# The edge stage of a four-layer convolution network: operators, normalisation and first convolution as one 5x5 convolution per image on raw input

## Chip, cores and metric

One core of one Trainium2 chip runs the kernel. The metric is the device time of one execution in microseconds. TensorE (PE) multiplies, VectorE (DVE), ScalarE (ACT) and GpSimd (POOL) work elementwise, SyncE (SP) issues most of the transfers.

## What is computed

The whole network maps x, 16 images of 32 channels of 128 x 128 float32, through four layers, each `x + layer(group_norm(x))`. The change touches the start of layer 3. There, v is the normalised x, and per image:

```
b1 = norm(sobel(v)); b2 = norm(scharr(v)); b3 = norm(laplace(v))
b4 = norm(roberts(v)); b5 = norm(prewitt(v))      # each channel by itself, reflect padding
y  = concat(b1..b5)                                # 160 channels
y  = conv3x3(y, conv1_w, conv1_b)                  # zero padding, 32 channels
y  = maxpool2(y)
...                                                # the hourglass, up to orig * y
def norm(x): return (x - mean(x)) / std(x)         # over channels, rows and columns of one image
```

## The kernel before, in words

`program` runs stages one after the other, each in a block of its own with a barrier at its end: per layer a `norm_table` (scale and shift of every channel of every image) and the layer's stages. What concerns us are the last five: `norm_table` "n2", `conv_layer` "l2" (layer 2, tensor names `l_`), `norm_table` "n3", `edges` ("l3a") and `hourglass` ("l3b"). Earlier stages give rows to compare: layer 0 (`l_mx`, `l_pv`), `state_space` (`l1m`), `tap_rows` (`l1y`), `deform` (`l1d`).

`norm_table` loads an image of 2 MB after the other (L74), takes statistics on VectorE (`bn_stats`, L87), and at the end one small matmul, a root and a store of the table (L76). GpSimd has nothing to do in it.

`edges` works through the 16 images in a hardware loop. Per image SyncE loads strips of 16 rows three times, shifted by one row each, onto 96 partitions (`xb`); ScalarE normalises them (`xn`, L1990 to L1994). TensorE makes the operator maps chunk by chunk of 4 rows: three matmuls with `w4` for four operators on 128 partitions (`p4`), three with `w5` for the fifth on 96 partitions (`p5`), L2103, 32 chunks. ScalarE and VectorE copy them to `r4` and `r5` (L2005, L2007, L2044, L2046) and VectorE takes statistics (L2047, L2049). After the last chunk comes a chain of small operations for mean and deviation; then ScalarE scales all of `r5` in place (L2018) and VectorE all of `r4` (L2079). Only then TensorE convolves: 8 steps of 12 taps, each tap four matmuls that write 32 partitions each side by side (L2118). VectorE takes the 2 x 2 maximum of each step (L2082), adds the bias (L2087), and SyncE stores the pooled rows. Every engine takes its instructions in the order in which they are written; semaphores are the only ordering between engines.

## Time and profile before

| | us |
|---|---|
| median of 3 runs | 24395.71 (24389.47 to 24419.06) |
| the profiled execution, its time | 24396.36 |
| its span, first to last instruction | 24394.8 |
| TensorE busy in the span | 19768.2 (81%) |
| VectorE busy | 15076.5 (62%) |
| ScalarE busy | 13799.3 (57%) |
| GpSimd busy | 8849.7 (36%) |

Busy shares are averages over stages that have different limits, so they have to be read stage by stage. Rows of the profile name line, engine, operation and "output <- inputs" with the tensors' names; PEld is TensorE loading weights, SPq and POOLq are queues of transfers, PEclk is the granted TensorE clock as a share of 2.4 GHz. Timeline rows begin with start and length in us. Sequences of "xN" are N instructions in a row.

### The profile page before, as it was taken

The page shows a single profiled execution, that of the slowest core. Times are in us where ns is not written, and L with a number is a line of the kernel's source. Part 1 is how long each engine was busy: PE and PEld are TensorE (multiplying, and loading weights), DVE is VectorE, ACT ScalarE, POOL GpSimd, SP SyncE. Part 2 cuts the span into 40 slices and gives each one's busy share as a digit, 9 for nine tenths or more (in the row PEclk, how much of TensorE's full clock was granted, in tenths as well). Part 3 has the DMA queues.
Part 4 walks back from the last instruction along what each step waited for, and adds up shares of the span by engine and source line. Part 5 has one row for each costly group of instructions (what it writes and reads, how often), then busy time and mean ns, then how long its engine had stood idle before and what let it go on. Part 6 is the DMA issues. An engine that isn't in the chain of part 4 may idle for free. (4 is left out here: it accounts for less than half of the span.)

```text
span 24394.8 us, 385684 instructions
## 1 busy us (share of the span) xinstructions
PE 19768.2 (81%) x135184; PEld 8014.9 (33%) x135184; DVE 15076.5 (62%) x15737; ACT 13799.3 (57%) x22826; POOL 8849.7 (36%) x5553
## 2 busy tenths in 40 slices
PE   6888888886438888888868999994468888888999
PEld 2333333332112222222215555551123333333444
DVE  8999999998138888888855666564143333333011
ACT  6889999896336666666636877783322222222111
POOL 6777778785017777777750000000000000000000
PEclk9999999998769999999988998797789999999999
DMA  1000000001950000000022111126920000111011
GB/s 65 11 12 12 11 12 12 12 11 64 158 116 18 18 18 18 18 17 18 18 69 35 34 34 37 30 38 151 198 71 23 23 23 23 29 24 30 31 43 43
DMA packets 1301498, 995.53 MB, mean 41 GB/s; under 512 B 748392, under 2 KB 1157584, under 8 KB 1265112
## 3 DMA queue, kind: packets, MB, share of 16 engines
q1 hardware_dynamic: 1199560, 849.64, 16.3%
q0 software_dynamic: 26624, 100.67, 1.5%
q10 hardware_dynamic: 74448, 33.14, 0.5%
q8 instruction: 608, 9.96, 0.2%
q14 instruction: 258, 2.11, 0.0%
HBM read 771.60 MB, written 211.63 MB: 40 GB/s over the span
## 5 line engine op out<-in xcount | busy, mean ns | idle before, releaser
L270 DVE TENSOR_TENSOR l_mx<-l_p_v,l_puN 128x2048 f32<-128x2048 f32 x2560 | 5636.5, 2282 | 151.6 <-PE l_p_s L485 138.7
L485 PE MATMUL l_p_s<-l_mx,l_w2z 128*32 128x512 f32 x32768 | 3827.9, 611 | 579.8 <-ACT l_mx L397 315.3
L290 POOL TENSOR_TENSOR l_mx<-l_pv,l_puP 128x2048 f32<-128x2048 f32 x1024 | 3715.6, 3644 | 321.8 <-PE l_p_s L485 316.0
L2103 PE MATMUL l3a_p<-l3a_xn,l3a_w 128*128 128x512 f32 (+1 forms) x6144 | 2680.9, 599 | 271.1 <-ACT l3a_xn L1994 271.1
L1157 DVE TENSOR_TENSOR_SCAN l1m_hs<-l1m_da,l1m_carry,l1m_pu 128x512 f32<-128x512 f32 x2304 | 2824.4, 1268 | 105.9 <-ACT l1m_da L1073 2.2
L2209 POOL DMA_DIRECT2D l3b_xt<-x_after x64 | 33.9, 529 | 7644.3 <-DVE l3b_most L2338 5818.0
L1206 POOL TENSOR_TENSOR l1m_hc<-l1m_hs,l1m_cs 128x1024 f32<-128x1024 f32 x1152 | 2708.7, 2351 | 9.2 <-DVE l1m_hs L1157 5.7
L1815 ACT ACTIVATE l1d_ab<-l1d_pt 128x1024 f32<-128x1024 f32 x2304 | 2299.4, 1024 | 706.9 <-PE l1d_pt L1569 693.0
L416 ACT ACTIVATE l_mx<-l_pv,l_puP 128x128 f32<-128x128 f32 x8192 | 2446.8, 393 | 0.8
L1693 DVE TENSOR_SCALAR l1d_hat<-l1d_ab 128x1024 f32<-128x1024 f32 x2304 | 1623.0, 704 | 818.9 <-ACT l1d_ab L1815 516.4
L397 ACT ACTIVATE l_mx<-l_mx 128x2048 f32<-128x2048 f32 x1024 | 1954.4, 1909 | 49.5 <-POOL l_mx L290 48.9
L485 PEld LDWEIGHTS l_p_s<-l_mx,l_w2z 128*32 128x32 f32 x32768 | 984.6, 112 | 3020.9 <-issue 1760.6
L1147 DVE TENSOR_TENSOR l1m_pu<-l1m_pu,l1m_bs 128x512 f32<-128x512 f32 x2304 | 1477.5, 687 | 749.3 <-PE l1m_pu L902 749.0
L1073 ACT ACTIVATE l1m_da<-l1m_pr,l1m_an 128x512 f32<-128x512 f32 x2304 | 1457.2, 683 | 823.4 <-PE l1m_pr L895 772.8
L902 PE MATMUL l1m_pu<-l1m_dts,l1m_sl 32*128 32x512 f32 x4608 | 1420.7, 692 | 534.8 <-ACT l1m_da L1073 525.9
L2231 PE MATMUL l3b_ps<-l3b_in,l3b_wc 128*128 (+2 forms) x3888 | 1638.2, 583 | 127.7 <-DMA l3b_in<-pooled 102.9
L2103 PEld LDWEIGHTS l3a_p<-l3a_xn,l3a_w 128*128 128x128 f32 (+1 forms) x6144 | 1094.1, 178 | 1857.9 <-issue 1857.9
L1604 PE MATMUL l1d_po<-l1d_hat,l1d_ring 128*32 128x128 f32 x36864 | 1640.6, 300 | 49.8 <-DVE l1d_hat L1693 45.8
L2118 PE MATMUL l3a_pc<-l3a_r,l3a_c 128*32 128x512 f32 x12288 | 1357.7, 605 | 270.7 <-issue 270.7
L1877 POOL TENSOR_TENSOR l1d_res<-l1d_res,l1d_xr 128x512 f32<-128x512 f32 x128 | 168.7, 1319 | 3540.6 <-ACT l1d_res L1824 3540.6
L895 PE MATMUL l1m_pr<-l1m_dts,l1m_sl 32*128 32x512 f32 x4608 | 1407.8, 689 | 2.7 <-ACT l1m_da L1073 2.7
L2005 ACT ACTIVATE l3a_r<-l3a_p 128x512 f32<-128x512 f32 x512 | 306.3, 598 | 1810.2 <-PE l3a_p L2103 1810.2
(301 smaller groups left out, 26624.6 us busy)
## 6 DMA issues: line engine op xcount, KB each, us to landing
n_xt<-x_after SPq DMA_DIRECT2D x48, 2048.0 KB
l3a_xb<-x_after SPq DMA_DIRECT2D x352, 256.0 KB, 4.1
...
l1m_sq<-seq SPq DMA_DIRECT2D x256, 144.0 KB
...
l_xs<-in_x_dram SPq DMA_DIRECT2D x128, 256.0 KB, 2.9
x_after<-l_ot SPq DMA_DIRECT2D x128, 256.0 KB, 2.4
```

The lines of the kernel that those rows point to most:

```text
L270: v.tensor_tensor(mx[:, r % QB, :, :, :], columns.unsqueeze(1).broadcast_to([P, 4, G, P]), rows.broadcast_to([P, 4, G, P]), ALU.max).then_ ...
L290: g.tensor_tensor(mx[:, r % QB, :, :, :], pv[:, u, :, :].unsqueeze(1).broadcast_to([P, 4, G, P]), rows.broadcast_to([P, 4, G, P]), ALU.add ...
L397: act.activation(tile, tile, ACT.Relu).then_inc(max_by_g, 1)
L416: ins = act.activation(mx[:, r % QB, q, t, :], pv[:, u, t, :], ACT.Relu, bias=puP[:, u, t, R * q + r:R * q + r + 1])
L485: ins = pe.matmul(p_s[R * q:R * (q + 1), 512 * u:512 * (u + 1)], w2z[:, 31 - r:63 - r], mx[:, r % QB, q, :, :].rearrange("p t v -> p (t v) ...
L1157: dve.tensor_tensor_scan(hs[:, p % 3, part, :], da[:, p % 3, part, :], pu[:, LC * bank:LC * (bank + 1)], carry[:, u, c:c + 1], ALU.mult, A ...
L1206: g.tensor_tensor(hc[:, (3 * u + p) % 6], hs[:, p % 3], cs[:, u:u + 1, :].broadcast_to([NB, 2, LC]), ALU.mult).then_inc(hc_done, 2)
L1604: ins = pe.matmul(po[C * g:C * (g + 1), 512 * (s % 2):512 * (s % 2) + P], ring[:, (8 * u + s + k) % RING, g, k, :], hat[:, m % 3, n % 2, P ...
L1693: v.tensor_scalar(hat[:, m % 3], ab[:, m % 2], 1.0, 1.0, ALU.min, ALU.subtract).then_inc(hat_done, 1)
L1815: act.activation(ab[:, m % 2].rearrange("p a n -> p (a n)"), pt[:, 1024 * (m % 2):1024 * (m % 2 + 1)], ACT.Abs).then_inc(abs_done, 1)
L2103: ins = pe.matmul(acc[0:n, 512 * (ch % 2):512 * (ch % 2 + 1)], w[:, dx, :], xn[:, k % 2, r:r + RC, dx:dx + W], start=dx == 0, stop=dx == 2)
L2231: ins = pe.matmul(bank(name, u, rows * size), wc[:, k, tap, :], src[:, at((i + u) * rows + tap // 3, rows), tap % 3:tap % 3 + size], start ...
```

## The change

Normalising the maps and convolving them is linear, and so are the operators, so all of it is one 5 x 5 convolution of the raw x per image, with taps that depend on the image through five standard deviations and the scale of x. Per image the taps are a weighted sum of five fixed tap tensors, one per operator.

- `norm_table` gets an option: GpSimd makes the fixed taps out of `conv1_w` and operator coefficients while the table is computed, three operators in "n2", two in "n3", and SyncE stores them (`folded`, 49 matrices of 32 columns per operator).
- `edges` is written anew. `xs` holds the raw image four times, shifted by 0 or 1 row and 0 or 1 column, so that a matmul over 128 partitions covers 2 x 2 taps: nine matmuls, four abreast, make a step (`pc`, 8 steps per image). Pixels of the outer rim follow other taps and are computed apart in `bb` (`border`), copied to `side` and `ends`, and put in place of the rim of each step before the maximum.
- The statistics of the five maps no longer fall out of TensorE's maps. They come from the *next* image beside the convolution of this one: its rows are loaded in strips (`xe`), 4 rows of each quarter on 128 partitions, normalised by ScalarE (`xn`), differenced by GpSimd (`tv`, `th`, `tp`, `t1`, `t2`, `te`, `tg`) and VectorE (`td`, `tf`, `t3`), made into five maps by VectorE with their sums, and squared by ScalarE with sums of the squares. Eight chunks make an image.
- After the last chunk: one small matmul, a root, and VectorE's `weights`, which forms the image's 49 matrices (`wb`, 1568 columns).

The core of the diff (loads of weights, the rim's matmuls and copies, and what is removed are left out; the removed part is `edges` as printed above):

```diff
+                g.wait_ge(f_in, 32)
+                step = 0
+                for i in range(F):
+                    for t in range(9):
+                        weight = ft[:, i, t, :].unsqueeze(1).broadcast_to([P, ROUNDS, T])
+                        coef = fc[:, i, t, :].unsqueeze(2).broadcast_to([P, ROUNDS, T])
+                        g.tensor_tensor(fv[:, i] if t == 0 else fp[:, t % 2], weight, coef, ALU.mult).then_inc(f_step, 1)
+                        step += 1
+                        if t > 0:
+                            g.wait_ge(f_step, step)
+                            g.tensor_tensor(fv[:, i], fv[:, i], fp[:, t % 2], ALU.add).then_inc(f_step, 1)
+                            step += 1
+
         @block.tensor
...
+def edges(nc, x, table, folded, taps, valid, mean_image, bias, out, B):
...
+            def strips(i, c):
+                n = i * NB + c
+                if not (isinstance(n, int) and n < 2):
+                    sp.wait_ge(xn_ready, n - 1)
...
+            def refill(i, k):
+                if not isinstance(i, int) or i > 0:
+                    sp.wait_ge(conv_done, i * NB + (min(max(k + 1, 2), NB - 1) + 1 - NB))
...
+            def once(b, u, follows, two_follow):
+                after, second = b + 1, b + 2
+                if follows:
+                    for c in range(2, 6):
+                        strips(after, c)
+                    refill(after, 0)
+                    strips(after, 6)
+                    refill(after, 1)
+                    strips(after, 7)
+                    refill(after, 2)
+                    if two_follow:
+                        strips(second, 0)
+                    refill(after, 3)
+                    if two_follow:
+                        strips(second, 1)
+                    for k in range(4, NB):
+                        refill(after, k)
...
+            def normalised(i, c, p):
+                n, u = i * NB + c, c % 2
+                if c == 0:
+                    act.wait_ge(g_ready, i + 1)
+                act.wait_ge(xe_in[u], xe_arrived(i, c))
+                if not (isinstance(n, int) and n < 2):
+                    act.wait_ge(pool_chunk, n - 1)
+                    act.wait_ge(dve_chunk, n - 1)
+                scale, shift_ = gcur[:, p, 0:1], gcur[:, p, 1:2]
+                act.activation(xn[:, u, :, 1:W + 1], xe[:, u], ACT.Identity, scale=scale, bias=shift_)
+                act.activation(xn[:, u, :, 0:1], xe[:, u, :, 1:2], ACT.Identity, scale=scale, bias=shift_)
+                act.activation(xn[:, u, :, W + 1:W + 2], xe[:, u, :, W - 2:W - 1], ACT.Identity, scale=scale, bias=shift_).then_inc(xn_ready, 1)
...
+            def squares(i, c):
+                u = c % 2
+                act.wait_ge(dve_chunk, i * NB + (c + 1))
+                for o in range(OPS):
+                    ins = act.activation(maps[:, u, o, :], maps[:, u, o, :], ACT.Square, accum_out=acc[:, OPS + o, c:c + 1])
+                ins.then_inc(sq_done, 1)
...
+            def once(b, u, follows, two_follow):
+                for k in range(5, NB):
+                    fix(b, k)
+                if follows:
+                    squares(b + 1, 0)
+                    normalised(b + 1, 2, 1 - u)
+                    squares(b + 1, 1)
+                    normalised(b + 1, 3, 1 - u)
+                border(b, u)
+                if follows:
+                    for c in range(2, 5):
+                        squares(b + 1, c)
+                        normalised(b + 1, c + 2, 1 - u)
+                    fix(b + 1, 0)
+                    squares(b + 1, 5)
+                    normalised(b + 1, 7, 1 - u)
+                    fix(b + 1, 1)
+                    squares(b + 1, 6)
+                    fix(b + 1, 2)
+                    squares(b + 1, 7)
+                    if two_follow:
+                        normalised(b + 2, 0, u)
+                        normalised(b + 2, 1, u)
+                    deviation(b + 1)
+                    fix(b + 1, 3)
+                    fix(b + 1, 4)
...
+            def chunk(i, c):
+                n, u = i * NB + c, c % 2
+                px = lambda dy, dx, rows=CR: xn[:, u, 1 + dy:1 + dy + rows, 1 + dx:1 + dx + W]
+                g.wait_ge(xn_ready, n + 1)
+                if not (isinstance(n, int) and n < 1):
+                    g.wait_ge(pool_chunk, n)
+                g.tensor_tensor(tv[:], px(1, 0), px(-1, 0), ALU.subtract)
+                g.tensor_tensor(th[:], px(0, 1), px(0, -1), ALU.subtract).then_inc(pool_first, 1)
+                if not (isinstance(n, int) and n < 2):
+                    g.wait_ge(dve_chunk, n - 1)
+                g.tensor_tensor(tp[:, u], px(-1, -1, CR + 1), px(-1, 0, CR + 1), ALU.add)
+                g.tensor_tensor(t1[:, u], px(-1, -1), px(1, 1), ALU.add)
+                g.tensor_tensor(t2[:, u], px(-1, 1), px(1, -1), ALU.add)
+                g.wait_ge(pool_first, n + 1)
+                g.tensor_tensor(te[:, u], tv[:], th[:], ALU.add)
+                g.tensor_tensor(tg[:, u], th[:], tv[:], ALU.subtract).then_inc(pool_chunk, 1)
...
+            def chunk(i, c):
+                n, u = i * NB + c, c % 2
+                px = lambda dy, dx: xn[:, u, 1 + dy:1 + dy + CR, 1 + dx:1 + dx + W]
+                to = lambda o: maps[:, u, o, :].rearrange("p (y x) -> p y x", x=W)
+                v.wait_ge(xn_ready, n + 1)
+                if not (isinstance(n, int) and n < 1):
+                    v.wait_ge(dve_chunk, n)
+                v.tensor_tensor(td[:], px(1, 1), px(-1, -1), ALU.subtract)
+                v.tensor_tensor(tf[:], px(-1, 1), px(1, -1), ALU.subtract)
+                v.wait_ge(pool_chunk, n + 1)
+                v.tensor_tensor(t3[:], t1[:, u], t2[:, u], ALU.add).then_inc(dve_first, 1)
+                if not (isinstance(n, int) and n < 2):
+                    v.wait_ge(sq_done, n - 1)
+                v.scalar_tensor_tensor(out=to(3), in0=tp[:, u, 0:CR], scalar=-1.0, in1=tp[:, u, 1:CR + 1], op0=ALU.mult, op1=ALU.add,
+                                       accum_out=acc[:, 3, c:c + 1])
+                v.wait_ge(dve_first, n + 1)
+                v.scalar_tensor_tensor(out=to(0), in0=td[:], scalar=1.0, in1=te[:, u], op0=ALU.mult, op1=ALU.add, accum_out=acc[:, 0, c:c + 1])
+                v.scalar_tensor_tensor(out=to(1), in0=td[:], scalar=0.6, in1=te[:, u], op0=ALU.mult, op1=ALU.add, accum_out=acc[:, 1, c:c + 1])
+                v.scalar_tensor_tensor(out=to(2), in0=px(0, 0), scalar=-4.0, in1=t3[:], op0=ALU.mult, op1=ALU.add, accum_out=acc[:, 2, c:c + 1])
+                v.scalar_tensor_tensor(out=to(4), in0=tf[:], scalar=2.0, in1=tg[:, u], op0=ALU.mult, op1=ALU.add,
+                                       accum_out=acc[:, 4, c:c + 1]).then_inc(dve_chunk, 1)
...
+            def weights(i, p):
+                v.wait_ge(dev_ready, i + 1)
...
+                v.tensor_scalar(wb[:, p, :], fv[:, 0, :], coef[:, 0:1], None, ALU.mult).then_inc(chain, 1)
...
+                for o in range(1, OPS):
+                    v.wait_ge(chain, i * CHAIN + (7, 8, 10, 11)[o - 1])
+                    ins = v.scalar_tensor_tensor(out=wb[:, p, :], in0=fv[:, o, :], scalar=coef[:, o:o + 1], in1=wb[:, p, :],
+                                                 op0=ALU.mult, op1=ALU.add).then_inc(w_ready if o == OPS - 1 else chain, 1)
...
+            def pool(b, k):
+                bank = pc[:, 512 * (k % 4):512 * (k % 4 + 1)]
+                v.wait_ge(conv_done, b * NB + (k + 1))
...
+                rows = bank.rearrange("p (y x) -> p y x", x=W)
+                v.tensor_copy(rows[:, :, 0:W:W - 1], side[:, k]).then_inc(replaced, 1)
...
+                v.tensor_reduce(pooled[:, k, :].rearrange("p (a w) -> p a w", w=W // 2),
+                                bank.rearrange("p (a dy x dx) -> p a x dy dx", a=CR // 2, dy=2, dx=2), AX.XY, ALU.max).then_inc(pool_done, 1)
...
+            def once(b, u, follows, two_follow):
+                if two_follow:
+                    choose(b + 2, u)
+                if follows:
+                    for c in range(4):
+                        chunk(b + 1, c)
+                for k in range(4):
+                    pool(b, k)
+                    if follows:
+                        chunk(b + 1, 4 + k)
+                pool(b, 4)
+                if follows:
+                    totals(b + 1)
+                pool(b, 5)
+                if follows:
+                    spread(b + 1)
+                    weights(b + 1, 1 - u)
+                pool(b, 6)
+                pool(b, 7)
+                v.wait_ge(pool_done, b * NB + NB + 4)
...
+            def step(b, u, k):
+                pe.wait_ge(fixed, b * NB + (k + 1))
+                pe.wait_ge(pool_done, b * NB + (k + 1))
+                rounds = rounds_of(KINDS[0])
...
+                        r, j = 16 * k + CR * g + by + 2, bx + 2
+                        ins = pe.matmul(pc[C * g:C * (g + 1), 512 * (k % 4):512 * (k % 4 + 1)], weight(u, n), xs[:, r:r + CR, j:j + W],
+                                        start=n == 0, stop=n == len(rounds) - 1, tile_position=(0, C * g))
...
+            def once(b, u, follows, two_follow):
+                pe.wait_ge(w_ready, b + 1)
+                step(b, u, 0)
+                step(b, u, 1)
+                border(b, u)
+                for k in range(2, 6):
+                    step(b, u, k)
+                if follows:
+                    total(b + 1)
+                step(b, u, 6)
+                step(b, u, 7)
```

Of GpSimd before, from the end of `deform` on, the whole list up to `hourglass`: none of it lies in the edge stage. Below, its last elementwise work, in `deform`, as the list of before has it, and then the transfers of `hourglass`:

```order
L1877 TENSOR_TENSOR l1d_res<-l1d_res,l1d_xr 128x512 x3
L1883 TENSOR_TENSOR l1d_finished<-l1d_eps 128x1
L1866 DMA x_after<-l1d_res 128x16x128
L1430 UNCONDITIONAL_BRANCH
L24 ISA x5
L2203 UNCONDITIONAL_BRANCH
L2205 UNCONDITIONAL_BRANCH
L2206 UNCONDITIONAL_BRANCH
L2206 ISA
L2209 ISA
L2209 DMA l3b_xt<-x_after 128x1024
```

Now, in the edge stage, one chunk (there are 8 per image; `l3a_xn` is the normalised strip):

```order
L2203 TENSOR_TENSOR l3a_tv<-l3a_xn 128x512
L2204 TENSOR_TENSOR l3a_th<-l3a_xn 128x512
L2207 TENSOR_TENSOR l3a_tp<-l3a_xn 128x640
L2208 TENSOR_TENSOR l3a_t<-l3a_xn 128x512
L2209 TENSOR_TENSOR l3a_t<-l3a_xn 128x512
L2211 TENSOR_TENSOR l3a_te<-l3a_tv,l3a_th 128x512
L2212 TENSOR_TENSOR l3a_tg<-l3a_th,l3a_tv 128x512
```

GpSimd received seven two-input operations per chunk, all from SBUF.

VectorE in the edge stage before, one chunk of 4 rows (32 per image; `l3a_p` is PSUM):

```order
L2044 COPY l3a_r<-l3a_p 32x4x128
L2046 COPY l3a_r<-l3a_p 32x4x128
L2047 BN_STATS l3a_parts<-l3a_p 32x6
L2048 REGISTER_ALU
L2049 BN_STATS l3a_parts<-l3a_r 128x6
```

Now VectorE in the loop over images, one pooling of this image and one chunk of the next:

```order
L2297 COPY l3a_pc<-l3a_side 128x4x2
L2304 REGISTER_ALU
L2305 TENSOR_REDUCE l3a_pooled<-l3a_pc 128x128
L2242 REGISTER_ALU
L2245 TENSOR_TENSOR l3a_td<-l3a_xn 128x512
L2246 TENSOR_TENSOR l3a_tf<-l3a_xn 128x512
L2248 TENSOR_TENSOR l3a_t<-l3a_t 128x512
L2251 SCALAR_TENSOR_TENSOR l3a_maps,l3a_acc<-l3a_tp 128x512
L2254 SCALAR_TENSOR_TENSOR l3a_maps,l3a_acc<-l3a_td,l3a_te 128x512
L2255 SCALAR_TENSOR_TENSOR l3a_maps,l3a_acc<-l3a_td,l3a_te 128x512
L2256 SCALAR_TENSOR_TENSOR l3a_maps,l3a_acc<-l3a_xn,l3a_t 128x512
L2257 SCALAR_TENSOR_TENSOR l3a_maps,l3a_acc<-l3a_tf,l3a_tg 128x512
```

The copies out of PSUM are gone; eight operations with both inputs in SBUF stand in their place, and the poolings moved in between them.

ScalarE before, two of the 32 chunks of an image, the copies of the maps out of PSUM:

```order
L2005 ACTIVATE l3a_r<-l3a_p 128x4x128
L2007 ACTIVATE l3a_r<-l3a_p 32x4x128
L2002 REGISTER_ALU
L2005 ACTIVATE l3a_r<-l3a_p 128x4x128
L2007 ACTIVATE l3a_r<-l3a_p 32x4x128
```

Now ScalarE where one image's statistics end and the next one's begin: squares of chunk 6, the columns of one refill (`xs`), squares of chunk 7, chunk 0 of the image after:

```order
L2127 ACTIVATE l3a_maps,l3a_acc<-l3a_maps 128x512 x5
L2139 ACTIVATE l3a_xs<-l3a_xs 64x16x2 x2
L2125 REGISTER_ALU
L2127 ACTIVATE l3a_maps,l3a_acc<-l3a_maps 128x512 x5
L2113 REGISTER_ALU
L2114 ISA
L2116 ISA
L2119 ACTIVATE l3a_xn<-l3a_xe,l3a_gcur 128x6x128
L2120 ACTIVATE l3a_xn<-l3a_xe,l3a_gcur 128x6
L2121 ACTIVATE l3a_xn<-l3a_xe,l3a_gcur 128x6
```

The copies are gone, and the squares of chunk 7 stand ahead of the normalisation of the next image's chunk 0.

## Rows read from the trace of the kernel before

**Rows 1.** The page, busy time of each engine, share of the span, instructions

```profile
PE 19768.2 (81%) x135184; PEld 8014.9 (33%) x135184; DVE 15076.5 (62%) x15737; ACT 13799.3 (57%) x22826; POOL 8849.7 (36%) x5553
```

**Rows 2.** Windows: a `norm_table`, part of `conv_layer`, the edge stage

```profile
core 0: us, PE busy (x) PEld busy (x) DVE busy (x) ACT busy (x) POOL busy (x), PEclk, DMA share, GB/s
16661.00:16790.00 129.00, 0.61 (x2) 0.50 (x2) 82.86 (x154) 0.31 (x1) 0.00 (x0) 0.50 0.70 261
17250.00:17350.00 100.00, 43.56 (x371) 11.64 (x364) 11.26 (x15) 34.28 (x22) 0.00 (x0) 0.73 1.11 207
...
17801.00:22472.00 4671.00, 4052.64 (x18496) 1537.88 (x18496) 1682.93 (x2499) 1167.79 (x1488) 0.00 (x0) 0.93 0.10 24
```

**Rows 3.** Groups of the edge stage by form: busy us, mean ns, idle before

```profile
L2103 PE MATMUL l3a_p<-l3a_xn,l3a_w 128*128 128x512 f32 x3072 | 1441.7, 606 | 271.1 <-ACT l3a_xn L1994 271.1
L2103 PE MATMUL l3a_p<-l3a_xn,l3a_w 128*96 128x512 f32 x3072 | 1403.7, 593 | 0.0
L2118 PE MATMUL l3a_pc<-l3a_r,l3a_c 128*32 128x512 f32 x12288 | 1357.7, 605 | 270.7 <-issue 270.7
...
L2018 ACT ACTIVATE l3a_r<-l3a_r,l3a_sc 96x16128 f32<-96x16128 f32 x16 | 221.5, 13844 | 0.0
L2079 DVE TENSOR_SCALAR l3a_r<-l3a_r,l3a_sc 128x16384 f32<-128x16384 f32 x16 | 141.0, 8815 | 0.6
L2082 DVE TENSOR_REDUCE l3a_pooled<-l3a_pc 128x128 f32<-128x512 f32 x128 | 88.6, 692 | 1385.8 <-PE l3a_pc L2118 1385.8
```

**Rows 4.** Timeline, first and last rows of the edge stage: start us, us

```profile
17801.11 0.69 DVE L2028 MEMSET l3a_w<- 128x384 f32 x2 [9.65 <-PEq L25]
...
17850.00 0.17 DVE L2034 TENSOR_SCALAR l3a_gcur<-l3a_gn 96x2 f32 x1 [8.08 <-DMA l3a_gn<-norm_table]
...
17857.38 5.46 PE L2103 MATMUL l3a_p<-l3a_xn,l3a_w 128*128 128x512 f32 x6 [67.41 <-ACT l3a_xn L1994]
...
22465.60 0.69 DVE L2082 TENSOR_REDUCE l3a_pooled<-l3a_pc 128x128 f32<-128x512 f32 x1 [9.61 <-PE l3a_pc L2118]
...
22471.93 0.38 SPq L2186 DMA_DIRECT2D l3b_wc<-in_w_convs_dram  x1
```

**Rows 5.** GpSimd's two-input operations by line: duration ns min/median/max

```profile
L1877 POOL TENSOR_TENSOR l1d_res<-l1d_res,l1d_xr x128: 1259/1281/1507, 13227.0 to 16652.4; 128x512 f32<-128x512 f32 x128
...
L1206 POOL TENSOR_TENSOR l1m_hc<-l1m_hs,l1m_cs x1152: 2334/2351/2377, 7203.4 to 12443.0; 128x1024 f32<-128x1024 f32 x192
...
L290 POOL TENSOR_TENSOR l_mx<-l_pv,l_puP x1024: 3630/3644/3674, 154.7 to 5918.2; 128x2048 f32<-128x2048 f32 x171
```

**Rows 6.** VectorE by line, two SBUF inputs, then a scaling

```profile
L2377 DVE TENSOR_TENSOR l3b_xt<-l3b_xt,l3b_ht x64: 1224/1225/1226, 22738.9 to 24389.7; 128x1024 f32<-128x1024 f32 x64
...
L2087 DVE TENSOR_SCALAR l3a_po<-l3a_pooled,l3a_bc x16: 752/754/755, 18132.9 to 22466.4; 128x1024 f32<-128x1024 f32 x16
```

**Rows 7.** ScalarE by line

```profile
L397 ACT ACTIVATE l_mx<-l_mx x1024: 1892/1910/1936, 161.5 to 5922.8; 128x2048 f32<-128x2048 f32 x171
...
L351 ACT ACTIVATE l_h<-l_xs,l_gn x256: 583/588/602, 142.3 to 5869.1; 128x256 f32<-128x256 f32 x128
...
L1993 ACT ACTIVATE l3a_xn<-l3a_xn x128: 232/232/235, 17856.8 to 22324.7; 96x16 f32<-96x16 f32 x128
```

**Rows 8.** Timeline of `tap_rows`, VectorE beside GpSimd, other engines left out

```profile
12508.35 1.22 DVE L1368 TENSOR_SCALAR l1y_v<-l1y_v 72x2048 f32<-72x2048 f32 x1
...
12508.78 4.71 POOL L1297 TENSOR_TENSOR l1y_r<-l1y_r,l1y_piece 72x2048 f32<-72x2048 f32 x1 [2.09 <-ACT l1y_piece L1316]
...
12509.60 4.97 DVE L1373 TENSOR_SCALAR l1y_y<-l1y_v 72x2048 f32<-72x2048 f32 x1
...
12517.31 4.07 POOL L1292 TENSOR_TENSOR l1y_r<-l1y_y,l1y_piece 72x2048 f32<-72x2048 f32 x1 [3.82 <-ACT l1y_piece L1314]
...
12517.91 2.29 DVE L1364 TENSOR_TENSOR l1y_v<-l1y_acc,l1y_base 72x2048 f32<-72x2048 f32 x1 [3.34 <-PE l1y_acc L1344]
```

**Rows 9.** Timeline, the store that ends the `norm_table` ahead of `conv_layer`

```profile
16781.18 0.41 SPq L76 DMA_DIRECT2D norm_table<-n_out  x1
```

512 lines of the change are left out of this document (300 added, 212 removed).

## Prediction

> **What bounds the kernel now.** I read the page first: TensorE is busy 81% of the span [rows 1]. Such a share is an average, so I cut the span into stages [rows 2]. The edge stage lasts 4671 us; in it TensorE is busy 4053 us, VectorE 1683, ScalarE 1168, GpSimd 0. The groups of that stage [rows 3] show what fills it: 6144 operator matmuls (1442 and 1404 us by form, overlap between the forms counted twice), 12288 convolution matmuls that run four abreast (1358 us, so 0.44 us per four), and, with TensorE idle, 13.8 us of normalisation per image beside a VectorE pass of 8.8 us. So **TensorE's instruction count and a serial chain per image** set the stage, (22465.6 - 17857.4) / 16 = 288 us an image [rows 4]. The stages before it, the two `norm_table` calls, last 129 us each [rows 2].
>
> **The change part by part.** The sum is made against the profiled execution's own 24396.4 us, 0.7 us over the median.
>
> *Removed.* All of the edge stage, first row to the first row of `hourglass`: 22471.9 - 17801.1 = 4670.8 us [rows 4].
>
> *TensorE after.* Per image 8 steps of 9 rounds, each four abreast: 72 x 0.44 = 32 us, and a rim of 76 small matmuls, about 5 us. From idle six matmuls took 5.46 us, 0.91 each [rows 4], twice the warm price; even so at most 75 us an image. No longer the bound.
>
> *GpSimd after.* Per chunk seven operations, six of 512 and one of 640 elements. It costs 1.28 us at 512 and 2.35 at 1024 [rows 5], so 640 is 1.55 and a chunk 9.2 us, 74 us an image. These rows read dense operands; the new ones read 128-element rows with a pitch of 130, which no row shows.
>
> *VectorE after.* 0.69 us at 512 and 1.225 at 1024 elements [rows 3, 6]: eight operations a chunk, 5.5 us; after GpSimd has finished the chunk six of them remain, 4.2 us. Five also write a sum: extra between nothing and 0.17 us each, a smallest operation [rows 4]; I take nothing and keep 0.8 us a chunk for the range. The weights of an image: one scaling of 1568 elements, 1.04 us (between 0.75 at 1024 and 8.8 at 16384), four of 1.79 us (1.225 + 544 x 1.04 ns), a dozen small at 0.17: 10.2 us. The Trainium skill ("VectorE: DVE Perf Modes", section "Two Vector instructions with no wait between them") says that an operation that also writes its accumulator is two instructions; by it the range's upper end would be the nearer one. No row here has such an operation.
>
> *ScalarE after.* Per chunk five squares at about 0.7 us (between 0.59 at 256 and 1.91 at 2048) and a normalisation of 768 elements with two edge columns, 1.4 us [rows 7]; with hand-overs 5.2 us.
>
> *Does VectorE run beside GpSimd?* This decides. In [rows 8] a GpSimd operation of about 4.1 us (the same form 4.07 below) began at 12508.78 while a VectorE scaling from SBUF to SBUF ran, and took 4.71. The next scaling, 1.22 us alone, began at 12509.60 and ended at 12514.57, which is 1.08 us behind GpSimd's end at 12513.49. **Each held the other off for nearly its whole length**; only some 0.2 us of GpSimd's and 0.14 us of VectorE's fixed part passed meanwhile. The last two of these rows are the counter-example: VectorE's 2.29 us addition with one input in PSUM ran inside a GpSimd operation unstretched. The new VectorE operations all read two operands from SBUF. No row has that form beside GpSimd. A scaling moves 1024 elements in 0.70 us, more than one a cycle of the 1.225 us form, so it too must use a second SBUF stream; that is why I take the first pair of rows as nearest. Of what passes meanwhile, a contended pair of operations costs 1.06 + 0.55 = 1.6 us. The Trainium skill ("SBUF — State Buffer", section "Who interferes with whom") says that a VectorE instruction with two SBUF inputs and a GpSimd one that reads SBUF exclude each other for the whole instruction, the later one waiting. By it the sum below stands, without it that of the second case.
>
> *The loop.* `xn` has two buffers: chunk c+2 is normalised only after VectorE has done chunk c and ScalarE has squared it. From GpSimd's end of an even chunk: six contended pairs 9.7, ScalarE 5.2, so chunk c+2 starts 14.9 us later (GpSimd finished c+1 at 11.8). It then meets three VectorE operations: 9.2 + 3 x 0.55 = 10.9. Two chunks per 25.8 us.
>
> *Between images.* Let T be GpSimd's end of chunk 7. In ScalarE's order the next image's chunk 0 stands behind the squares of chunk 7: 4.2 + 3.5 + 1.6, so GpSimd starts again at T+9.3. ScalarE's second normalisation and root end at T+11; VectorE's weights, with five big operations each held once by 1.06 us, at T+26.5; two poolings (0.69 and copies) and the bias, T+29.5; its chunk 0 with four contended, T+39.3; ScalarE, so GpSimd's chunk 2 starts at T+44.5. Chunk 2 ends at 54.8, 4 starts at 69.7, 6 at 95.5, 7 ends at **T+118**; I add 2 for what has no row and take 120 us. PE's steps, the refills and their waits fit inside: step 3 of an image is done by T+60, where its pooling stands behind the next image's chunk 3.
>
> *DMA.* 8.4 MB an image in 512-byte rows and 3.1 MB of strips. `conv_layer` moves the same kind of rows at 207 GB/s [rows 2]: 56 us an image, under 120. The last two refills wait for convolution step 7 and land about 12 us later. In SP's queue the strips of chunk 2 stand behind the stores, which wait for the bias at T+29.5; they land about T+36 and are needed at T+42. So no transfer ends a wait.
>
> *The stage.* Loads and the 180 small matmuls until VectorE starts, 25 us; its chunk 0, ScalarE, then six chunks, T of image 0 at 113. 15 x 120 = 1800. Tail: weights T+19, convolution 45 with the lower clock at first, last pooling and store 4, 5 for the stage's end: 73. Together **1986 us**.
>
> *The folding in `norm_table`.* An operator costs 9 products and 8 sums of 1568 elements on GpSimd: products as in the broadcast form, 3.64 x 1568/2048 = 2.79 us, sums about 3.4 [rows 5], 53 us with waits. Three operators 159 us from 16668, ending at 16827 where the table was stored at 16781 [rows 9], plus a 2.4 MB store: +50 us. Two operators, 106 us, hide under the 119 us of loads; their load and store add 8. VectorE's statistics beside it read one SBUF input, which I take as free. **+58 us** (40 to 80).
>
> 24396.4 - 4670.8 + 1986 + 58 = **21770 us**.
>
> **The rivals.** *Held off* (the forecast), 21770: 21650 to 21950 as the contended pair costs 1.5 to 2.0.
> *No exclusion:* the loop is 9.3 us a chunk, chunk 2 starts at T+35, the period is 93, the start 92: 92 + 1395 + 73 = 1560, in all **21343**. For it: the two-input form isn't in the trace. Against: the held scalings.
> *Longer chain:* fully serial pairs (2.0), accumulator reads on VectorE and ScalarE (0.17 each) and a table switch for the root make two chunks 30 us and the turn between images 10 longer: period 145, **22145**. For it: all of these lie in the loop, nothing hides them.
> *Slower than before:* GpSimd on rows of pitch 130 runs as many short rows, not one. The kernel breaks even at a period of 295 us, which is 4.5 us instead of 1.28 for each of its 56 operations an image; at 4.6 us about 24480. Against: `l_mx` rows with broadcast views cost less than dense ones [rows 5].
>
> **How the numbers follow.** Held off 0.70, no exclusion 0.15, longer chain 0.13, slower 0.02. The time is the first's. The range 21320 to 22160 takes in the first, nearly all of the second and half of the third. 0.2% (49 us), about what a measurement here can tell, decides nothing: faster 0.98, same 0, slower 0.02.
>
> **What would show it.** The edge stage's span near 1990; GpSimd busy most there and VectorE beside it longer than 0.69 us per operation (held); 0.69 and 1.28 flat would be the second case. GpSimd idle before `tv` for ScalarE, about 9 and 9 us at the turn. TensorE's clock low and its share near a third. `n2` about 50 us longer, `n3` about 8. I'm wrong if strips or refills end the waits, or if the turn between images is far from 45 us.

## The result, and the profile after

The changed kernel takes 21,707 us (median of 4, 21,677 to 21,728), before 24,407 us (median of 4, 24,389 to 24,473); the ratio is 0.889 (95% interval 0.888 to 0.891). The forecast was 21,770 us. The profiled execution took 21,728.42 us; all stage times below are its own, or those of the experiment's own profiled execution.

The first fence is the page's line of busy times (as [rows 1]) and windows over the edge stage (as the last of [rows 2]; columns as there).

```profile
PE 16948.3 (78%) x128728; PEld 6960.4 (32%) x128728; DVE 14936.5 (69%) x15487; ACT 13323.2 (61%) x23402; POOL 10513.1 (48%) x6534
...
core 0: us, PE busy (x) PEld busy (x) DVE busy (x) ACT busy (x) POOL busy (x), PEclk, DMA share, GB/s
17892.06:19804.61 1912.55, 1194.84 (x12040) 466.45 (x12040) 1533.13 (x2249) 686.17 (x2064) 1392.20 (x896) 0.81 0.56 106
```

The stage fell from 4671 to 1912.5 us (first row 17892.06, first row of `hourglass` 19804.61). TensorE's share of it went from 87% to 62%, VectorE's from 36% to 80%, GpSimd's from nothing to 73%. The next fence shows groups of that stage by form (columns as [rows 3]).

```profile
L2368 PE MATMUL l3a_pc<-l3a_xs,l3a_wb 128*32 128x512 f32 x9216 | 1107.0, 640 | 245.3 <-DVE l3a_pooled L2305 217.2 <-DVE l3a_wb L2283 26.6 <-ACT l3a_xs L2139 1.4
...
L2211 POOL TENSOR_TENSOR l3a_te<-l3a_tv,l3a_th 128x512 f32<-128x512 f32 x128 | 221.5, 1731 | 0.0
...
L2203 POOL TENSOR_TENSOR l3a_tv<-l3a_xn 128x512 f32<-128x512 f32 x128 | 217.7, 1701 | 441.7 <-ACT l3a_xn L2121 432.6
...
L2246 DVE TENSOR_TENSOR l3a_tf<-l3a_xn 128x512 f32<-128x512 f32 x128 | 188.8, 1475 | 0.0
...
L2255 DVE SCALAR_TENSOR_TENSOR l3a_maps<-l3a_td,l3a_te 128x512 f32<-128x512 f32 x128 | 174.6, 1364 | 0.0
...
L2283 DVE SCALAR_TENSOR_TENSOR l3a_wb<-l3a_fv,l3a_coef,l3a_wb 128x1568 f32<-128x1568 f32 x64 | 172.5, 2696 | 1.1
...
L2209 POOL TENSOR_TENSOR l3a_t<-l3a_xn 128x512 f32<-128x512 f32 x128 | 170.7, 1333 | 0.0
...
L2254 DVE SCALAR_TENSOR_TENSOR l3a_maps<-l3a_td,l3a_te 128x512 f32<-128x512 f32 x128 | 129.0, 1008 | 0.0
...
L2248 DVE TENSOR_TENSOR l3a_t<-l3a_t 128x512 f32<-128x512 f32 x128 | 88.5, 691 | 157.6 <-POOL l3a_tg L2212 157.6
...
L2305 DVE TENSOR_REDUCE l3a_pooled<-l3a_pc 128x128 f32<-128x512 f32 x128 | 88.5, 691 | 4.4
```

All seven GpSimd operations and all eight of VectorE in a chunk have the same work, 512 elements (`tp` 640), and yet their means run from 0.69 to 1.48 us on VectorE and from 1.33 to 1.73 on GpSimd. The timeline says when. Start and length in us, GpSimd in chunk 1 of image 0 and VectorE still in chunk 0, TensorE and ScalarE left out:

```profile
17917.58 1.73 DVE L2255 SCALAR_TENSOR_TENSOR l3a_maps<-l3a_td,l3a_te 128x512 f32<-128x512 f32 x1
17918.72 1.53 POOL L2208 TENSOR_TENSOR l3a_t<-l3a_xn 128x512 f32<-128x512 f32 x1
17919.24 0.08 DVE L2255 DVE_READ_ACCUMULATOR l3a_maps<-l3a_td,l3a_te 128x1 f32 x1
17919.24 1.57 DVE L2256 SCALAR_TENSOR_TENSOR l3a_maps<-l3a_xn,l3a_t 128x512 f32<-128x512 f32 x1
17920.22 1.54 POOL L2209 TENSOR_TENSOR l3a_t<-l3a_xn 128x512 f32<-128x512 f32 x1
...
17920.73 1.57 DVE L2257 SCALAR_TENSOR_TENSOR l3a_maps<-l3a_tf,l3a_tg 128x512 f32<-128x512 f32 x1
```

A VectorE operation with both inputs in SBUF, 0.685 us long and 0.61 us from start to start when nothing lies beside it, is drawn out to 1.5 to 1.7 us beside a GpSimd operation, and GpSimd's are drawn out by VectorE's (L2209 takes 1.54 here and 1.09 at 18156.41, with VectorE idle): they take turns, one pair each 1.5 to 1.66 us. The pooling (L2305) reads PSUM and stays at 0.69. The 77 ns row of the accumulator starts together with the next operation and lies inside the length of the one before it.

The loop and the turn between images, as GpSimd's rows show them (brackets: idle before, and what ended it):

```profile
18104.51 1.71 POOL L2212 TENSOR_TENSOR l3a_tg<-l3a_th,l3a_tv 128x512 f32<-128x512 f32 x1
18115.21 1.28 POOL L2203 TENSOR_TENSOR l3a_tv<-l3a_xn 128x512 f32<-128x512 f32 x1 [8.99 <-ACT l3a_xn L2121]
...
18150.94 1.78 POOL L2203 TENSOR_TENSOR l3a_tv<-l3a_xn 128x512 f32<-128x512 f32 x1 [12.25 <-ACT l3a_xn L2121]
...
18173.29 1.52 POOL L2203 TENSOR_TENSOR l3a_tv<-l3a_xn 128x512 f32<-128x512 f32 x1 [1.97 <-ACT l3a_xn L2121]
...
18197.15 1.54 POOL L2203 TENSOR_TENSOR l3a_tv<-l3a_xn 128x512 f32<-128x512 f32 x1 [1.97 <-ACT l3a_xn L2121]
```

T, GpSimd's end of an image's chunk 7, is 18104.51 + 1.71 = 18106.2 for image 1. GpSimd starts again 9.0 us later, chunk 2 at T+44.7. From chunk 2 to chunk 4 it is 22.4 us, from chunk 4 to chunk 6 18197.15 - 18173.29 = 23.9. From T of image 0 (17996.5) to T of image 15 (19704.3) it is 113.9 us an image.

| us | forecast | measured |
|---|---|---|
| first image, to T | 113 | 104.4 |
| period of an image | 120 | 113.9 |
| after T of image 15 | 73 | 100.3 |
| edge stage | 1986 | 1912.5 |
| n2 and n3 longer by | 50 + 8 | 45.8 + 5.0 |
| everything else | 0 | +40 |

The last row is `deform` (3456 against 3425 us, with a granted clock of 0.89 against 0.91 on average over it) and 7 us in front of it. No line there is changed. In the profiled executions of this study n2 starts between 16,633 and 16,754 us, before and behind the 16,661 of the kernel before, so this is scatter. So the experiments are compared by the length of their stages, not by their totals.

### The profile page after: what moved, and what is told of

Its sections match the earlier page's. It is cut to its first block and busy times, and to the rows that moved or that the text cites. A ratio compares the mean times of both kernels' runs of the same rounds, so it can differ in the third digit from the quotient of the medians.

```text
span 21726.9 us, 374304 instructions
## 1 busy us (share of the span) xinstructions
PE 16948.3 (78%) x128728; PEld 6960.4 (32%) x128728; DVE 14936.5 (69%) x15487; ACT 13323.2 (61%) x23402; POOL 10513.1 (48%) x6534
## 5 line engine op out<-in xcount | busy, mean ns | idle before, releaser
L1639 PE MATMUL l1d_pg<-l1d_wz,l1d_im 32*128 32x288 f32 x5120 | 1280.2, 576 | 69.7 <-DVE l1d_ring L1733 26.5
L2368 PE MATMUL l3a_pc<-l3a_xs,l3a_wb 128*32 128x512 f32 x9216 | 1107.0, 640 | 245.3 <-DVE l3a_pooled L2305 217.2
L1657 PEld LDWEIGHTS l1d_po<-l1d_hat,l1d_ring 128*32 128x32 f32 x36864 | 956.3, 117 | 754.9 <-issue 637.2
L2521 PEld LDWEIGHTS l3b_ps<-l3b_in,l3b_wc 128*128 128x128 f32 x3888 | 725.4, 190 | 1041.9 <-issue 1026.2
L1733 DVE COPY l1d_ring<-l1d_pg 128x288 f32<-128x288 f32 x1280 | 582.3, 455 | 653.4 <-PE l1d_pg L1639 651.1
```

The costliest lines, as they stand in the source:

```text
L1657: ins = pe.matmul(po[C * g:C * (g + 1), 512 * (s % 2):512 * (s % 2) + P], ring[:, (8 * u + s + k) % RING, g, k, :], hat[:, m % 3, n % 2, P ...
L2521: ins = pe.matmul(bank(name, u, rows * size), wc[:, k, tap, :], src[:, at((i + u) * rows + tap // 3, rows), tap % 3:tap % 3 + size], start ...
```

## The experiments

Stage: first row of the edge stage to the first of `hourglass`. Period: between the first scalings of `wb` of image 0 and 15, over 15.

| | stage | period | total |
|---|---|---|---|
| changed kernel | 1912.5 | 113.9 | 21,728 |
| e1_all_vector | 1734.6 | 103.1 | 21,550 |
| e2b_narrow | 1359.6 | 79.8 | 21,103 |
| e3_psum | 1794.3 | 106.6 | 21,557 |
| e4_order | 1936.3 | 115.4 | 21,713 |
| e5_four_xn | 1930.0 | 114.3 | 21,730 |
| e7_vector_pools | 1610.1 | 95.2 | 21,364 |
| e8_hybrid | 1473.3 | 86.5 | 21,294 |
| e9_bf16 | 1376.3 | 81.0 | 21,111 |

**Who holds whom.** First the seven GpSimd operations moved to VectorE:

```diff
-                g.tensor_tensor(tv[:], px(1, 0), px(-1, 0), ALU.subtract)
...
-                g.tensor_tensor(tg[:, u], th[:], tv[:], ALU.subtract).then_inc(pool_chunk, 1)
+                v.tensor_tensor(tv[:], px(1, 0), px(-1, 0), ALU.subtract)
...
+                v.tensor_tensor(tg[:, u], th[:], tv[:], ALU.subtract)
```

> Only change: GpSimd's seven operations of each chunk are issued by VectorE, behind td and tf. The changed kernel's edge stage lasts 1912 us, 114 us an image, with VectorE's two-input operations at 1.0 to 1.5 us beside GpSimd and 0.69 us without it. Theory (VectorE and GpSimd hold each other off): with nobody beside it each of the 15 operations starts 0.61 us after the one before, 9.3 us a chunk, 74 an image; poolings 6.5, weights 10.0, the wait for ScalarE and the small chain 6: period 97, stage about 1650, time about 21,450. Rival (the operations are long by themselves, for their sums or the pitch of 130): 15 x 1.2 = 18 us a chunk, period over 150, stage over 2500. Second rival (something else, TensorE at 75 us an image or the refills, ends the waits): period above 105 with VectorE idle.

Groups of its edge stage, an addition of the weights, `td`, and a map with its sum:

```profile
L2263 DVE SCALAR_TENSOR_TENSOR l3a_wb<-l3a_fv,l3a_coef,l3a_wb 128x1568 f32<-128x1568 f32 x64 | 118.4, 1850 | 1.1
...
L2217 DVE TENSOR_TENSOR l3a_td<-l3a_xn 128x512 f32<-128x512 f32 x128 | 87.9, 687 | 5.6
L2234 DVE SCALAR_TENSOR_TENSOR l3a_maps<-l3a_td,l3a_te 128x512 f32<-128x512 f32 x128 | 87.7, 685 | 0.0
```

All fourteen operations of 512 elements take 0.683 to 0.687 us, with the sum or without, with the pitch of 130 or without: the operations aren't long by themselves. VectorE now issues fifteen operations in place of eight and the stage is 178 us **shorter**: what takes GpSimd 1.0 to 1.3 us alone takes VectorE 0.61, and while GpSimd did it, VectorE had mostly been held. The period is 103, not 97: as in the second rival, though less than it asked for, VectorE waits for another engine. The waits of this run show it idle for convolution step 7 (85.4 us in 14 images, 6 each) and TensorE for poolings. That is taken up in e7.

Then the opposite, GpSimd's part made tiny:

```diff
-                px = lambda dy, dx, rows=CR: xn[:, u, 1 + dy:1 + dy + rows, 1 + dx:1 + dx + W]
+                px = lambda dy, dx, rows=CR: xn[:, u, 1 + dy:1 + dy + rows, 1 + dx:2 + dx]
```

> Part of the computation left out: GpSimd's seven operations of a chunk work on one column of 128, so the maps are not complete (their buffers are set to zero once, before the loop); VectorE, ScalarE, TensorE and all transfers do the same work as in the changed kernel. It prices GpSimd's share of the 114 us an image and shows what lies under it. Theory (held off): VectorE's two-input operations are 0.69 us nearly everywhere, weights' additions 1.85 instead of 2.7; a chunk is bound by ScalarE's 5.2 us, statistics and weights would take about 75 us, and TensorE's 75 to 80 us of steps and rim becomes the bound: period about 85, stage about 1450. Rival (VectorE's operations are long for another reason, GpSimd merely follows): VectorE's rows keep 1.0 to 1.5 us and the period stays above 105.

Of VectorE's groups for the operations of a chunk, the longest and the shortest:

```profile
L2261 DVE SCALAR_TENSOR_TENSOR l3a_maps<-l3a_xn,l3a_t 128x512 f32<-128x512 f32 x120 | 82.9, 691 | 0.0
...
L2256 DVE SCALAR_TENSOR_TENSOR l3a_maps<-l3a_tp 128x512 f32<-128x512 f32 x120 | 82.2, 685 | 0.0
```

VectorE's rows were 0.685 to 0.691 us, the weights' additions 1.850; period 79.8, where 85 was expected. So GpSimd's work costs 34 us of the 114, and under it lies a floor at 80 us in which TensorE is busy 83%. (e2_narrow, the same without the zeros in the buffers, gave no time.)

**Which VectorE operations are held.** Two operands moved to PSUM:

```diff
-        td = m.sb("td", [P, CR, W])
-        tf = m.sb("tf", [P, CR, W])
+        td = m.bank("td")[:, :].rearrange("p (y x) -> p y x", x=W)
+        tf = m.bank("tf")[:, :].rearrange("p (y x) -> p y x", x=W)
```

> Only change: td and tf, each used as one of two inputs by three of the five map operations (maps 0, 1 and 4), lie in two free PSUM banks instead of SBUF. Theory (only an operation with both inputs in SBUF needs what GpSimd uses): the operations for maps 0, 1 and 4 (L2254, L2255, L2257 of the changed kernel, 1.01, 1.36 and 1.30 us on average) become 0.69 to 0.75 us flat and GpSimd's beside them 1.27, while td, tf and maps 2 and 3 stay at 1.0 to 1.5; a pair of chunks takes about 19.5 us instead of 23.9, period about 99, stage about 1680. Rival (any VectorE operation is held while GpSimd runs, or the sums cost the time): all rows keep their lengths, stage 1912 within 20.

Groups of its stage: the three maps that read PSUM, and, for contrast, one that reads two SBUF operands, and `tf`.

```profile
L2246 DVE TENSOR_TENSOR l3a_tf<-l3a_xn 128x512 f32<-128x512 f32 x124 | 184.4, 1487 | 0.0
...
L2256 DVE SCALAR_TENSOR_TENSOR l3a_maps<-l3a_xn,l3a_t 128x512 f32<-128x512 f32 x124 | 150.4, 1213 | 0.0
...
L2254 DVE SCALAR_TENSOR_TENSOR l3a_maps<-l3a_td,l3a_te 128x512 f32<-128x512 f32 x124 | 84.6, 682 | 0.0
L2257 DVE SCALAR_TENSOR_TENSOR l3a_maps<-l3a_tf,l3a_tg 128x512 f32<-128x512 f32 x124 | 84.6, 682 | 0.0
L2255 DVE SCALAR_TENSOR_TENSOR l3a_maps<-l3a_td,l3a_te 128x512 f32<-128x512 f32 x124 | 84.5, 682 | 0.0
```

The three fell to 0.682; `tf` and maps 2 and 3 stayed at 1.2 to 1.5, `td` at 0.97 (1.05 before). That GpSimd holds every VectorE operation is excluded, and so is a price of the sums, which the three write as well. What is held reads two operands from SBUF; `td` and `tf` are still held although their output is in PSUM. The period came to 106.6 and not 99: two chunks took 20.9 us instead of the 19.5 given, with GpSimd now busy without a gap over 0.2 us through the loop (held by the four VectorE operations `td`, `tf` and maps 2 and 3; `t3` begins before GpSimd's next operation and takes 0.70). Its rows were not 1.27 flat as expected, `tv`, `te` and `tg` kept 1.7. At the turn the weights, all SBUF, are held as before (L2283, 2.695 us against 2.696).

**Is GpSimd's idle time on the path?** ScalarE's order at the turn:

```diff
-                    squares(b + 1, 7)
                     if two_follow:
                         normalised(b + 2, 0, u)
+                    squares(b + 1, 7)
+                    if two_follow:
                         normalised(b + 2, 1, u)
```

> Only change: in ScalarE's list the normalisation of the next image's chunk 0 stands ahead of the squares of chunk 7, so GpSimd no longer waits 9.0 us for it at the turn between images. Theory (VectorE's chain through maps, squares, weights and the next chunk 0 sets the turn, and GpSimd's fourteen operations of two chunks cost it the same wherever they fall beside it): GpSimd's idle time before tv of chunk 0 falls to about 3 us, VectorE's maps of chunk 7 become longer instead, and the idle time before chunk 2 grows by as much; period 114 within 2, stage 1912 within 30. Rival (GpSimd's idle time is on the path): 6 us an image less, stage about 1820.

GpSimd's first row of chunk 0 behind the turn, its last of chunk 1, and its wait before chunk 2:

```profile
18534.44 1.56 POOL L2204 TENSOR_TENSOR l3a_tv<-l3a_xn 128x512 f32<-128x512 f32 x1 [2.54 <-ACT l3a_xn L2121]
...
18554.43 2.82 POOL L2213 TENSOR_TENSOR l3a_tg<-l3a_th,l3a_tv 128x512 f32<-128x512 f32 x1
18579.00 1.79 POOL L2204 TENSOR_TENSOR l3a_tv<-l3a_xn 128x512 f32<-128x512 f32 x1 [21.75 <-ACT l3a_xn L2121]
```

The wait before chunk 0 fell from 9.0 to 2.5 us, and the one before chunk 2 rose from 12.25 to 21.75 (in every second image from about 15.5 to 23.5). Together that is 24.3 us of waiting instead of 21.2: nothing was gained, the period grew by 1.5. Next, two more buffers of `xn`:

```diff
-        xn = m.sb("xn", [P, 2, CR + 2, W + 2])
+        xn = m.sb("xn", [P, 4, CR + 2, W + 2])
...
-                if not (isinstance(n, int) and n < 2):
-                    act.wait_ge(pool_chunk, n - 1)
-                    act.wait_ge(dve_chunk, n - 1)
+                if not (isinstance(n, int) and n < 4):
+                    act.wait_ge(pool_chunk, n - 3)
+                    act.wait_ge(dve_chunk, n - 3)
```

> Only change: four buffers of xn instead of two, with strips and normalisations issued two chunks earlier. My prediction built the loop on the two buffers: GpSimd waits 2.0 us before every even chunk, 9.0 and 12.3 us at the turn. Theory A (the two engines' mutual holding is the capacity: fourteen pairs of operations at about 1.54 us and the rest at 0.61 fill 23 of the 23.9 us of a pair of chunks whatever the buffers): the waits for xn vanish from GpSimd, it runs ahead and then waits for VectorE's previous chunk (te, tg and the sums have two buffers); period 110 to 114, stage 1850 to 1912. Theory B (the two-buffer chain costs what GpSimd is idle, 6 + 9 + 12 us an image): period about 90, stage about 1550.

The waits of its stage:

```profile
engine line waited for: us in total, times, longest us
...
ACT l3a_maps L2129 <- DVE l3a_maps L2265: 486.7, 73, 11.3
POOL l3a_tp L2215 <- DVE l3a_maps L2265: 369.3, 89, 27.4
```

No wait for `xn` is left among them; GpSimd waits for VectorE's last map instead (`te`, `tg`, `t1`, `t2` and `tp` have two buffers), and the period is 114.3, stage 1930, both slightly over the ranges given. From 18,000 to 19,140 us VectorE is busy 92% of the time, against 84% in the changed kernel. Together e4 and e5 say that the chain through the two buffers of `xn`, on which my loop was built, describes when things happen and not what they cost; VectorE, lengthened by GpSimd, fills the period without it. With more buffers everywhere GpSimd could run further ahead; that wasn't tried.

**What remains with one engine, and a better kernel.** Poolings one chunk earlier, the sum over partitions after step 7, the folding over four tables:

```diff
-                    for c in range(4):
+                    for c in range(3):
                         chunk(b + 1, c)
-                for k in range(4):
+                for k in range(5):
...
-    norm_table(nc, "n0", x0, tables[0], a["pair_mean"], B)
+    norm_table(nc, "n0", x0, tables[0], a["pair_mean"], B, (e_taps, a["e_coef"], folded, (0,)))
```

> Three changes. (1) All fifteen operations of a chunk on VectorE, as in e1_all_vector, where the period was 103.1 us. (2) The poolings of an image stand one chunk earlier in VectorE's list, so that pooling 7 comes before the weights, and TensorE's sum over partitions stands behind step 7: in e1_all_vector VectorE waited 6 us for convolution step 7 and TensorE up to 5 us for a pooling. (3) The folding is spread over four norm_tables, operators 0, 1, 2 and 3 with 4 in n0, n1, n2 and n3. If VectorE alone is the bound, its rows add up to 15 x 0.61 + 0.13 = 9.3 x 8 = 75 for the chunks, 6.7 poolings, 9.7 weights, 0.8 bias, 3 of waits for ScalarE and 1.2 of issue: period 96 to 98, stage about 1640. If TensorE or the refills bind, the period stays at 103. The folding: n2 lasts 174.4 us in the changed kernel with three operators and 129 without; now 133 to 136, and n0 and n1 4 to 7 us more each, so 30 us less in all. Time about 21,420.

Period 95.2, one below the range given; VectorE waits for TensorE nowhere, only 1.6 and 1.2 us an image for ScalarE. n2 lasts 129.7 us with one operator where three made 174.4, n3 131.9; in n0 the store of the table is issued at 119.5 us as in the changed kernel (119.4), and the next stage starts 1.7 us later; n1 lasts 130.5 us against 128.8. So the spreading took 45 us off n2 for 3.4 us in n0 and n1: some 41 of the 51 us that the folding cost were to be had back.

Then GpSimd gets back only what fits beside VectorE's reads of PSUM:

```diff
+                g.wait_ge(free, 2 * n)
+                g.tensor_tensor(tv[:], px(1, 0), px(-1, 0), ALU.subtract)
+                g.tensor_tensor(th[:], px(0, 1), px(0, -1), ALU.subtract).then_inc(pool_first, 1)
```

> Built on e7_vector_pools (period 95.2 us, all of it VectorE's own work). Change: td and tf in PSUM as in e3_psum; tv and th go back to GpSimd; map 2 stands ahead of maps 0, 1 and 4, and GpSimd starts tv of the next chunk only when map 2 is done, so that its two operations (2.3 us) meet VectorE's maps 0, 1 and 4, which read one operand from PSUM (1.9 us), and the pooling (0.85 us, from PSUM). Theory (only VectorE's operations with both inputs in SBUF are held): VectorE issues 13 operations, 1.22 us less a chunk, 9.8 an image, and no row of it is longer than 0.70 except td or tf in the three chunks without a pooling behind them: period 86 to 88, stage about 1500, time about 21,230. Rival (GpSimd beside VectorE costs it about as much as it takes over, as in the changed kernel): period 95 or more.

Groups of its stage: GpSimd's two, and VectorE's longest:

```profile
L2204 POOL TENSOR_TENSOR l3a_tv<-l3a_xn 128x512 f32<-128x512 f32 x112 | 143.9, 1285 | 952.3 <-DVE l3a_maps L2253 768.5 <-ACT l3a_xn L2122 183.8
L2205 POOL TENSOR_TENSOR l3a_th<-l3a_xn 128x512 f32<-128x512 f32 x112 | 116.7, 1042 | 0.0
...
L2238 DVE TENSOR_TENSOR l3a_td<-l3a_xn 128x512 f32<-128x512 f32 x111 | 84.9, 765 | 3.3
...
L2255 DVE SCALAR_TENSOR_TENSOR l3a_maps<-l3a_td,l3a_te 128x512 f32<-128x512 f32 x112 | 76.7, 685 | 0.0
```

GpSimd's two are at their lengths without a neighbour (1.27 and 1.04 us in the first chunk of the changed kernel, where VectorE hadn't begun), and of VectorE's thirteen only `td` is longer than in e1 by more than 0.01 us, by 0.08 on average. Period 86.5, within the 86 to 88 that was stated: the two operations, placed so, save 8.7 us an image.

Last, 16 bits for what the statistics read:

> Built on e7_vector_pools (period 95.2 us, VectorE bound). Change: what the statistics read and form on the way (xn, tv, th, te, tg, t1, t2, tp, td, tf, t3) is kept in 16 bits; the maps, their squares and sums and the whole convolution stay in 32 bits. VectorE only adds and subtracts the same 15 operations. The Trainium skill (VectorE: DVE Perf Modes, the walkthrough of the modes) says that a two-input operation on 16-bit operands whose starts are aligned to 4 bytes passes two elements a cycle. Estimate if it holds for the ten plain two-input operations except tv and tp (their operands begin at odd elements): eight of them fall from 0.61 us apart to about 0.34, 2.2 us a chunk, 17 an image, and then TensorE's steps (75 to 80 us, period 79.8 in e2b_narrow) bind: period about 80, stage about 1390. If it doesn't hold, the period stays at 95.

To e7_vector_pools the edit appends `BF16` in the eleven buffers' declarations. Groups of its stage: a map with its sum, `tv` with odd starts, and an operation with aligned ones:

```profile
L2234 DVE SCALAR_TENSOR_TENSOR l3a_maps<-l3a_td,l3a_te 128x512 f32<-128x512 bf16 x109 | 74.9, 687 | 0.0
...
L2219 DVE TENSOR_TENSOR l3a_tv<-l3a_xn 128x512 bf16<-128x512 bf16 x109 | 46.1, 423 | 0.0
...
L2217 DVE TENSOR_TENSOR l3a_td<-l3a_xn 128x512 bf16<-128x512 bf16 x109 | 45.6, 419 | 2.9
```

All ten plain operations fell, `tv` too, whose operands both begin at odd elements (0.423 us against 0.419); the maps stayed at 0.69. The Trainium skill ("VectorE: DVE Perf Modes", section "Walkthrough: the 8-slice pipeline in each mode") asks for starts aligned to 4 bytes; here an odd start cost 4 ns. The period stops at 81.0, about the floor of e2b_narrow. In this run TensorE waits 11 us an image for `wb`, VectorE 4.3 for TensorE and 3.0 for the rim (13 images, 18,000 to 19,100 us): a ring of waits through weights, steps, refills and rim, whose costliest part I did not separate.

> The kernel of e8_hybrid again, timed against the kernel before. Its one execution took 21,294 us, the changed kernel's median is 21,707. Expected: the edge stage 1473 us as there, the two norm_tables 130 and 132 us, median 21,290 within 40, ratio to before 0.873, which is 1.9% under the changed kernel's 0.889.

> The kernel of e9_bf16 again (the statistics' operands in 16 bits), timed against the kernel before. Its one execution took 21,111 us in a faster run of the stages ahead of the change: measured from the start of n2 to the end it was ahead of e8_hybrid by about 97 us. Expected: the edge stage 1376 us, median 21,200 within 60, ratio 0.868.

Measured: e10 21,218 us (median of 4, 21,141 to 21,238), ratio 0.869 (0.867 to 0.871); e11 21,127 us (21,065 to 21,171), ratio 0.866 (0.864 to 0.868), each against 24,397 us. The periods were 86.5 and 81.1 as before; the medians came out 72 and 73 us under the expectations, outside their margins. The expectation of e10 rested on one execution of e8_hybrid in which n2 started at 16,754 us, 77 us later than in e10's profiled one. The one of e11 took e9_bf16's execution for a fast one and put 89 us on top, but n2 had started there at 16,668 us, and in e11's profiled one at 16,656. **e10 is 2.3% faster than the changed kernel with the same float32 operations.**

## Why the prediction was right, point by point

- *VectorE and GpSimd hold each other off.* Right, and it decided: the step from the scalings of [rows 8] to two-input operations held. A contended pair took 1.5 to 1.66 us (1.66 and 1.49 between the starts above), I had 1.6. The rival without exclusion, 21,343, is excluded by e1, e2b and e3. The Trainium skill ("SBUF — State Buffer", "Who interferes with whom") excludes by operands and not by engine; e3 shows that distinction.
- *The loop*, 25.8 forecast, 23.9 measured. After GpSimd's end I had charged six contended pairs, 9.7 us; it was five and a free one, since `t3` begins before GpSimd's next operation does: 8.4. ScalarE took 4.9, not 5.2. The number was near for a reason that was in part another: by e5 this chain is not what costs, since without its waits the period stayed at 114.3. The price is VectorE's own rows with GpSimd beside them, which come to nearly the same length.
- *The turn.* GpSimd again at T+9.3, measured 9.0; weights done at T+26.5, measured 27.4; chunk 2 at T+44.5, measured 44.7, and 48.1 in every second image. There VectorE stands 3.25 us at the jump of its loop over two images and 3.54 us again four operations into the next chunk (at 18,250.3 and 18,256.2 us), both with "issue" as the reason: no term of mine.
- *Sums.* Free on VectorE (0.685 with, 0.684 without) and on ScalarE (squares start 0.61 us apart). The end of my range that I took, nothing, was the nearer one. The two instructions of which the Trainium skill speaks ("VectorE: DVE Perf Modes", section "Two Vector instructions with no wait between them") are in the trace, but the second, 77 to 83 ns, cost no time.
- *Pitch of 130.* `tv` takes 1.27 us alone, as dense rows do; `th` 1.04 and `tp`, with 640 elements, 1.25 where I had 1.55. The slow rival had no ground.
- *Transfers*, which I named as a sign of being wrong, end no wait that counts: refills end 409 us of ScalarE's waits in the stage, but of TensorE's only 1.4 us were put down to the columns that ScalarE writes behind them; strips end 23.6 us, nearly all at the start.
- *TensorE: wrong by two.* I wrote "12288 convolution matmuls that run four abreast (1358 us, so 0.44 us per four)". Twelve taps x 4 x 8 steps x 16 images are 6144; the trace counts every float32 matmul of these twice, so a tap of four costs 0.88 us [rows 3] and the steps 72 x 0.88 = 63 us an image, not 32. Now x9216 for 72 x 4 x 16 = 4608 shows the same, and the operator matmuls are doubled too: what I called six matmuls in 5.46 us [rows 4] are three. My sign for it failed: TensorE's share was to be near a third and is 62%, at a granted clock of 0.81. Beside 114 us it was hidden, and my bound of 75 us an image was just reached (74 to 76 busy in the windows of an image). Steps and rim fill 66 of the 80 us of e2b's period, and the price is most of why the tail failed.
- *The tail*, 73 forecast, 100.3 measured. Weights were done at T+18.6 (19 forecast). TensorE's rows and the end:

```profile
19712.61 33.19 PE L2368 MATMUL l3a_pc<-l3a_xs,l3a_wb 128*32 128x512 f32 x288
19745.63 1.58 PE L2381 MATMUL l3a_bb<-l3a_xs,l3a_wb 128*32 128x32 f32 x96
...
19750.57 46.60 PE L2368 MATMUL l3a_pc<-l3a_xs,l3a_wb 128*32 128x512 f32 x429
...
19797.20 0.17 DVE L2297 COPY l3a_pc<-l3a_side 128x8 f32<-128x8 f32 x1 [6.85 <-PE l3a_pc L2368]
...
19797.74 0.69 DVE L2305 TENSOR_REDUCE l3a_pooled<-l3a_pc 128x128 f32<-128x512 f32 x1
...
19804.61 0.36 SPq L2476 DMA_DIRECT2D l3b_wc<-in_w_convs_dram  x1
```

  TensorE worked from 19712.6 to 19797 without a gap: four steps, the rim, six steps (429 of their 432 rows are in the line shown), the ten at 7.7 to 8.3 us each. The first two were steps 6 and 7 of image 14, which in TensorE's list stand behind the sum over partitions, and so behind VectorE's totals (TensorE had been idle 23.8 us until then). I had neither seen that nor had the price: image 15's convolution began at about T+25, 6 us after its weights were done, and took 68 us, where I had planned 45 for its eight steps and rim.
- *First image*, 113 against 104.4: loads took 11 us until ScalarE began and VectorE 16 instead of 25.
- *The folding*, 58 against 51. Products took 2.83 and sums 3.49 us, and the three operators ended 166.5 us after the stage's start, where the forecast had them (159 + 7); only the added store and n3's load cost less than I gave. What I had taken as free wasn't quite. In n2, from the changed kernel's groups:

```profile
L102 DVE BATCH_NORM_STATS2 n_parts<-n_xt 128x512 f32 x128 | 77.5, 679 | 37.8 <-DMA n_xt<-x_after 37.8
...
L112 DVE TENSOR_TENSOR n_mv<-n_sq,n_aggr 128x16 f32<-128x16 f32 x1 | 2.7, 2690 | 0.0
...
L116 DVE TENSOR_TENSOR n_sq<-n_gm 128x16 f32<-128x16 f32 x1 | 2.5, 2546 | 0.0
```

  BN_STATS with its one SBUF input kept its 0.68 us, but five operations of the chain at the end of the table, 0.17 to 0.18 us each in n3, took 2.5 to 2.9 us beside GpSimd operations of 2.83 and 3.49, and the table came 15 us later. The folding hid that, as it ended later still.

The total was good by luck too: -73 and -7 against +40 that no line of the change explains. Within the stage the fifteen periods and the first image came 92 and 9 us under the forecast and the tail 27 over it, so that the stage alone was forecast 4% high.
